# Attention steps of a decoder kernel: a sum moved ahead of two rests, a rank computation placed between a projection's halves, a rest moved behind the decayed scores

## The reference, cut to what matters

```python
qh = _xpos(q @ Wq, offset=0, inverse_scale=False)
kh = _xpos(k @ Wk, offset=0, inverse_scale=True)
vh = v @ Wv
scores = jnp.einsum('bld,bmd->blm', qh, kh) * mask[None, :, :]
return scores @ vh
...
x = _layernorm(x + _L0_xattn_ref(x, ctx_1024, ctx_1024, ...), axis=-1)
x = _layernorm(x + _L0_ffn_ref(x, ...), axis=-1)
```

## Time and profile before

| | |
|---|---|
| time, median of 3 runs | 1731.2 us (1730.51 to 1731.84) |
| profiled execution, its own time | 1730.88 us |
| its span, first to last instruction | 1729.0 us |
| mean granted TensorE clock | 0.983 of full speed |
| attention steps | about 525 to 1050 us |

### The profile page before, as it was taken

How to read it: one execution, slowest core, us unless ns; L and a number is a source line. 1 busy time by engine, 2 the same in 40 slices (tenths; PEclk the granted TensorE clock), 3 DMA queues, 4 the chain that set the end, 5 groups by cost and what they waited for, 6 DMA issues and landing times.

```text
span 1729.0 us, 38474 instructions
## 1 busy us (share of the span) xinstructions
PE 1652.4 (96%) x11286; PEld 1491.6 (86%) x11287; DVE 1329.0 (77%) x2688; ACT 953.1 (55%) x1643; POOL 872.1 (50%) x770
## 2 busy tenths in 40 slices
PE   7999986999998999999999998999999999999995
PEld 6777765998986888888888877999999999999995
DVE  6888867888885887777787788777777777777774
ACT  5888876777743334334334345555555655555562
POOL 1111125888961354355345353556566656656564
PEclk9999998999998999999999999999999999999998
DMA  4555556889954332332332344334544544545444
GB/s 150 190 189 189 189 194 219 247 265 258 274 202 145 110 132 100 111 136 99 111 132 99 114 150 119 62 59 88 117 93 98 112 95 103 104 97 112 93 99 116
DMA packets 149263, 240.78 MB, mean 139 GB/s; under 512 B 40960, under 2 KB 104640, under 8 KB 141008
## 3 DMA queue, kind: packets, MB, share of 16 engines
q1 hardware_dynamic: 122608, 203.58, 37.2%
q0 software_dynamic: 26592, 36.46, 11.9%
HBM read 132.30 MB, written 107.68 MB: 139 GB/s over the span
## 4 chain that ended last, share of the span: by engine, by line
PE 47%; DMA 8%; DVE 7%; issue 4%; DVEq 1%; SPq 1%; ACT 1%; POOL 1%; POOLq 0%; ACTq 0%
PE block_banks L3074 16%; PE block_banks L3124 9%; PE block_banks L2880 5%; PE block_banks L2965 4%; PE block_banks L2956 4%; DMA attention_x<-x 3%; PE block_banks L2978 3%; DMA more<-back_y,back_token 3%; PE block_banks L2911 2%; PE block_banks L2919 2%; PE block_banks L3067 1%; DMA back_xe<-sorted 1%; DVE back_sum_rows L2447 1%; PE block_banks L2868 1%; PE block_banks L2936 1%
## 5 line engine op out<-in xcount | busy, mean ns | idle before, releaser
L3074 PE MATMUL block_banks<-back_xe_T,back_w_split 128*128 128x256 f32 x3408 | 437.4, 285 | 2.2 <-DVE back_xe_T L2749 1.5
L3074 PEld LDWEIGHTS block_banks<-back_xe_T,back_w_split 128*128 128x128 f32 x3408 | 418.1, 192 | 2.6 <-issue 1.7
L2337 ACT ACTIVATE back_w_split<-back_w_gu 128x1024 fp32r x142 | 150.8, 1063 | 235.7 <-PE block_banks L3074 231.3
L2730 DVE TENSOR_TENSOR back_w_split<-back_w_gu,back_w_split 128x1024 fp32r<-128x1024 f32 x142 | 174.0, 1226 | 63.6 <-ACT back_w_split L2337 36.0
L3124 PE MATMUL block_banks<-back_w_down,back_he_T 128*128 x1680 | 213.1, 283 | 0.9 <-DVE back_w_down L2412 0.9
L2175 POOL DMA_INDIRECT sorted<-back_x,back_slot x128 | 139.6, 1090 | 141.8 <-DVE back_slot L2558 92.6
L3124 PEld LDWEIGHTS block_banks<-back_w_down,back_he_T 128*128 128x128 f32 x1680 | 206.6, 192 | 1.1 <-issue 1.1
L1573 PE MATMUL block_banks<-front_xn_T,front_w_in_parts 128*128 128x512 f32 x768 | 186.3, 398 | 2.5 <-DVE front_xn_T L1344 1.1
L2211 POOL DMA_INDIRECT acc<-back_y,back_token x71 | 112.3, 1581 | 139.5 <-DVE back_y L2768 136.0
L1573 PEld LDWEIGHTS block_banks<-front_xn_T,front_w_in_parts 128*128 128x128 f32 x768 | 142.5, 189 | 39.7 <-DVE front_conv L1337 7.5
L2218 POOL TENSOR_TENSOR back_he_T<-back_h,back_he_T 128x512 fp32r<-128x512 f32 x71 | 114.4, 1611 | 116.2 <-ACT back_he_T L2355 116.2
(11 more groups left out here) (290 smaller groups left out, 3457.6 us busy)
## 6 DMA issues: line engine op xcount, KB each, us to landing
back_xe<-sorted SPq DMA_DIRECT2D x72, 272.0 KB, 2.8
gate_T<-front_gate_T SPq DMA_DIRECT2D x16, 1024.0 KB, 4.9
xc_T<-front_xc_T SPq DMA_DIRECT2D x16, 1024.0 KB, 5.8
front_xc_in<-xc_T SPq DMA_DIRECT2D x16, 1024.0 KB, 7.2
front_gate_in<-gate_T SPq DMA_DIRECT2D x16, 1024.0 KB, 5.9
front_c_rep<-c_parts SPq DMA_DIRECT2D x128, 64.0 KB, 5.4
front_rows_in<-in_x SPq DMA_DIRECT2D x16, 512.0 KB, 7.7
x<-front_x SPq DMA_DIRECT2D x16, 512.0 KB, 3.1
```

The source lines that it names most:

```text
L2337: nc.scalar.activation(w_split[:, r, 0, m].unsqueeze(1), w_gu[:, bass.ds(e, 1), m], ACT.Copy).then_inc(w_high_ready, 1)
L2730: nc.vector.tensor_tensor(w_split[:, r, 1, m].unsqueeze(1), w_gu[:, bass.ds(e, 1), m], w_split[:, r, 0, m].unsqueeze(1).bitcast(F32), ALU. ...
L3074: op = nc.tensor.matmul(dst[:, part, c % 2 * WINDOW:(c % 2 + 1) * WINDOW], w_split[:, r, w_part, m, k * D_FF + c * P:k * D_FF + (c + 1) * ...
```

## The change

It reorders instructions on VectorE and TensorE, adds none and removes none. On VectorE `rest_c(a + 1)` goes from behind `add_bias` to behind `decay_scores`, and `sum_rows_of(a)` goes ahead of `rest_h_s(g, 1)` and `rest_h_s(g, 2)`, still behind `hidden(g, 2)`. On TensorE the query projection is written as two calls of one half each, with `rank(a - 2, 1)` between them instead of behind both.

```diff
--- before.py
+++ after.py
@@ -2660,8 +2660,6 @@
                     w_down_low(0)
                 if expert:
                     add_bias(g)
-                if attention and not is_at(a, GROUPS - 1):
-                    rest_c(a + 1)
                 near_end = is_at(expert and g, GROUPS - 2)
                 last = is_at(attention and a, GROUPS - 1)
                 ahead = attention is not None
@@ -2682,16 +2680,19 @@
                         w_down_low(1)
                 if attention:
                     decay_scores(a)
+                if attention and not is_at(a, GROUPS - 1):
+                    rest_c(a + 1)
                 if is_at(attention and a, 0):
                     constants()
                 if is_at(expert and g, 1):
                     w_down_low(4)
                 if expert:
                     hidden(g, 2, ahead)
+                if attention:
+                    sum_rows_of(a)
+                if expert:
                     rest_h_s(g, 1)
                     rest_h_s(g, 2)
-                if attention:
-                    sum_rows_of(a)
                 if near_end:
                     stats_of(a)
                 if expert:
@@ -2872,8 +2873,8 @@
                 pe.wait_ge(x1_loaded, 16 * (a + 1))
                 turn(x1, x1_turned)
 
-            def project(w, src, done, parts_before=None):
-                for half in range(2):
+            def project(w, src, done, parts_before=None, halves=(0, 1)):
+                for half in halves:
                     if parts_before is not None:
                         pe.wait_ge(parts_ready, parts_before + 2 * half + 2)
                     for n, (w_part, src_part, k) in enumerate(PASSES):
@@ -2887,9 +2888,10 @@
                 else:
                     pe.wait_ge(parts_ready, 8)
                 pe.wait_ge(x1_T_ready, KM * (a + 1))
-                project(w_q, x1_T, q_done)
+                project(w_q, x1_T, q_done, halves=(0,))
                 if not is_at(a, 1):
                     rank(a - 2, 1)
+                project(w_q, x1_T, q_done, halves=(1,))
                 if is_at(a, 1):
                     pe.wait_ge(sum_ready, 2)
                 else:
```

## The result

The changed kernel takes **1723.33 us** (median of 17 runs, 1719.61 to 1727.5), the kernel before 1731.29 us in the runs beside it. The ratio is 0.9949, 95% interval 0.994 to 0.9958: faster by half a per cent, 8.0 us. The forecast was 1725.6 us, 5.6 us faster, with a range down to 1723.8. The direction came out as forecast; the gain was larger than the range allowed.

The account below looks back on a forecast made before the run. TensorE, busy 1652.4 of 1729.0 us, was taken as the bound, so only its idle time could be won. 6.5 (13 intervals) + 0.5 - 1.4 (last step) = 5.6 us, giving 1725.6 us, range 1723.8 to 1729.4.

Parts of the forecast that it names:

- the first part: Opening section on what bounds the kernel: TensorE's waits in the attention steps, 6.85 us to win over 13 intervals.
- 6.85 us is what these steps can give: 13 attention intervals, 427.14 us together, against 13 times the 32.33 us interval taken as free of waits.
- 0.35 for waits that remain: Deduction from the 6.85 us for waits left in single steps of the 13 intervals, leaving 6.5 us.
- 0.2 for the keys: Last attention step's key projection wait on TensorE: 0.2 us gained.
- Rank between the halves: Query projection on TensorE: place's 0.78 us wait goes, keys gain 0.30 us per interval, the split costs 0.
- Rival 2: Splitting the query costs 0.39 us each time, 5.5 us in 14 steps: 1731.1 us; chance 0.08.
- Sum ahead of the rests: VectorE's sum follows attend, x1 is issued 0.35 us earlier, and its 0.30 us wait in the interval goes.
- Rival 1: x1 load bound by DMA traffic, not its issue, so only the key wait goes: 1729.1 us; chance 0.12.
- The first interval: The first x1 wait, 1.5 us, shrinks by what the sum gains: 0.3 us.
- Rest of the context rows: VectorE, behind the decayed scores: 1.23 us instead of 3.16, in idle time, worth nothing by itself.
- Rival 4: Rest of the context rows meets GpSimd's reads, takes 4.23 us, sum 0.6 us later: 1736.9 us; chance 0.05.
- The last step: Last attention step: rests come between sum and statistics, TensorE waits 1.4 us longer for x2, between 0 and 1.5.

Follow-up runs that it names:

- e6: Changed kernel with the rests kept ahead of the sum in the last attention step and "more" cleared ahead of the x1 load; ratio 0.9942 to the kernel before.
- e10: The same kernel as e6, timed again: 1722.93 us, ratio 0.9939 to the kernel before.
- e2: Kernel before with only the sum of rows moved ahead of the two rests of h: 1728.71 us, ratio 0.9977.
- e5: Kernel before with only the clearing of "more" issued ahead of SyncE's wait for the sum, so ahead of the x1 load: 1724.98 us, ratio 0.9961.
- e4: Changed kernel with the two rests kept ahead of the sum in the last attention step; ratio 0.9949 to the kernel before.
- e11: Kernel before with rank and sum of rows moved, the rest of the context rows left in its old place; ratio 0.9957.
- e3: Kernel before with only the rest of the context rows moved behind the decayed scores; ratio 1.0000.
- e1: Kernel before with only rank moved between the two halves of the query projection: 1727.66 us, ratio 0.9966.

## Why the prediction was wrong in size and right in kind

**The step that failed** is the one in the first part: "One of them, 601.40 to 633.73, took 32.33 us, with no wait flagged for DMA or parts", and from it "6.85 us is what these steps can give". No wait flagged was read as no wait. That interval still held the keys back 0.10 us (6.77 against the 6.67 of every interval with rank moved), the x1 transposes by 0.22 in all, the keys' 0.10 among them (28.52 against 28.30 in the best intervals of e6), and some 0.06 behind those. The waits that the view leaves out were in the very interval that served as the measure. The best intervals of e6 and e10 put the floor at 32.05 us or below, so the steps could give at least 427.14 - 13 x 32.05 = 10.5 us, and the change took 8.4 of them, where the prediction allowed 6.5. Put 32.05 for 32.33 into the prediction's own sum, with its 0.35 for waits that remain, and it gives 10.5 - 0.35 + 0.5 - 1.4 = 9.2 us, for a measured 8.0 (7.3 to 10.4 by the ratio's interval).

By the traces the attention steps alone gained 8.4 + 1.4 - 0.7 = 9.2 us, where the sum had 6.5 + 0.3 - 1.2 (its last step's 1.4 less 0.2 for the keys). That this meets the 9.2 above is luck: the 13 intervals took 1.7 us less than the mended floor allows, and the first interval and the last step, below, came out 1.1 and 0.5 us better than forecast. The medians differ by less because other parts of the program differ by up to 2 us between profiles.

**Rank between the halves**: right, and so is its price of about 0. The wait of place is gone, rank waits for nothing, and what is late next is TensorE itself. The value projection starts 3.00 us after the query instead of 2.89, but the x2 transposes at 5.88 instead of 5.85, so the split costs 0.03 us and not 0.11. What follows rank takes 0.08 us longer in either place: the query's second half 1.47 us (632.78 to 634.25) where the first takes 1.39, and before the value projection 2.96 us, where it now takes 2.88; in the trace the 0.08 us lies between its first two matmuls. Rival 2 is out.

**Sum ahead of the rests**: right in mechanism and in its 0.35 us (0.31 alone in e2). Rival 1, the load bound by its traffic, was half right: the transfer beside it costs the load 0.7 us (landing after 4.1 us, 3.4 in e5), but an earlier issue moves the transposes one for one (4.11 us behind it in both kernels).

**The first interval** was under-sized: 0.3 us forecast, 1.4 measured between the first two profiles. The load of x1 there took 5.41 to 6.07 us from issue to transposes in the four traces of kernels with the sum last and "more" behind the load, 4.08 to 4.80 in those of e2, e4, e11 and the three of the changed kernel, 4.02 in e6 and e10, and 4.85 in e5. The sum's edit moves the issue by only 0.2 to 0.4 us and the transposes by 1.0 or more. What else the load shares in that one place wasn't tried and stays open.

**Rest of the context rows**: right, worth nothing alone (e3) or with the others (e11), 1.2 us long in idle time. Rival 4 is out.

**The last step**: right in place and sign, 1.4 us forecast, 1.03 measured (e4). The rests put 1.20 us between sum and statistics (from 1009.58 to 1010.78 in the changed kernel; ahead of the sum they took 1.44, from 1017.87 to 1019.31, because the second waited 0.1 us for ScalarE's rounded copy, which is there already when they stand behind the sum), and the sum starts 2.00 us after attend's start there (1008.38 - 1006.38) instead of 2.19 in e4 (1009.91 - 1007.72), where the rests end after attend: 1.20 - 0.19 = 1.01.

**The range** left out the measured time by 0.5 us because its lower end was worked out with the same floor: it allowed for all of 6.85 and an unpaid last step, but not for the floor to be wrong. By the measurement alone that half microsecond can't be told from none (its end at 1723.8 is 7.5 us under the kernel before, and the interval reaches down to 7.3); the stretches of the traces show the error.

## What to carry to other kernels

A floor taken from the best interval of a trace is an upper bound on the floor: compare the offsets of each waiting instruction over all intervals, and ask of the best one, too, what its start follows. The floor of 32.05 us here is such a bound as well. Where two waits sit in one loop, each gain moves the other's issue with it if that issue hangs on the engine that gained, so the two add up instead of passing on. A transfer queued right behind the one that somebody waits for costs it time although it comes second; issue it ahead of the wait, and look at what it then stands beside.

## What the runs showed of the hardware that I had not expected

The rest of the context rows (two SBUF inputs, 128x1024) takes 1.22 us alone and 3.16 beside GpSimd's xpos sums; in e1, where those start earlier against it, it takes 2.52. It ends some 1.1 us behind the last of the sums in all of these, as one that waits for them and then runs. What was new is the other direction: a scatter's descriptor work on GpSimd that begins while that rest runs takes longer, mostly 1.8 to 1.9 us instead of 0.96, and in all thirteen traces it ends 0.83 to 0.86 us behind the end of the rest, as one that waits for it and then runs. In the kernel before, this was the first scatter behind the xpos sums in all 13 steps of the window (1.78 or 1.79 us); in the changed kernel that one is short again, and three scatters of the whole window are so long (1.77 to 1.92 us), each begun 0.1 to 0.3 us after a rest had started; in e3_rest_c it is one scatter in 12 of the 13 steps (1.90 to 1.92 us), begun 0.1 to 0.2 us after it. One of them, on GpSimd and on VectorE:

```profile
618.29 1.92 POOL L2175 DMA_INDIRECT sorted<-back_x,back_slot  x1 [0.30 <-issue]
```

```profile
618.17 1.22 DVE L2423 TENSOR_TENSOR attention_c_T<-attention_c_raw,attention_c_T 128x1024 fp32r<-128x1024 f32 x1
```

The Trainium skill (SBUF — State Buffer, section "Who interferes with whom") infers that descriptor generation is not hindered by a tensor_tensor; these rows differ from that, and the measurement decides. In this kernel nothing waits for it.

The 512 KB load of x1 by SyncE's queue landed 3.4 us after its issue (e5), and 4.1 us after it with a second 512 KB transfer issued 0.4 us behind it (the kernel before).
